# Loading and checking a GNN stack's first adjacency tiles in pieces, and reading the outcome of the check at the end

## The reference

```
layer 0: x <- norm(x + sum_k T_k(A) x w_k(node) + b(node)),  T_0 = 1, T_1 = A, T_2 = 2AA - 1,
         w_k(node) = sum_d emb[node, d] W[d, k],  b(node) = sum_d emb[node, d] bias[d],  d < 16
layer 1: x <- norm(x + relu(A relu(A x w1) w2))
layer 2: x <- norm(x + x ws + (A x) wn + bias)
layer 3: x <- norm(x + [x, Ax, 2AAx - x, Ax, 2AAx - x] W + bias)
```

## Time and profile before

| what | value |
|---|---|
| median of the runs | 1294.76 us |
| profiled execution: its own time / its span | 1295.21 us / 1293.3 us |
| TensorE matmul (PE) busy | 1258.5 us, 97% of the span |
| VectorE (DVE) busy | 729.9 us, 56% |
| ScalarE (ACT) busy | 239.8 us, 19% |
| GpSimd (POOL) busy | 62.0 us, 5% |
| first product with the adjacency starts | 20.18 us |
| mean granted TensorE clock | 0.997 |

### The profile page before, as it was taken

One profiled execution on the slowest core, in us unless ns is written; L12 is line 12 of the kernel. 1 busy time (PEld: TensorE's weight loads), 2 busy tenths in 40 slices (PEclk: granted clock), 3 DMA queues, 4 the chain that ended last, 5 costly groups with the idle time before them and its releaser, 6 DMA issues.

```text
span 1293.3 us, 16451 instructions
## 1 busy us (share of the span) xinstructions
PE 1258.5 (97%) x6048; PEld 1045.5 (81%) x6048; DVE 729.9 (56%) x1811; ACT 239.8 (19%) x427; POOL 62.0 (5%) x52
## 2 busy tenths in 40 slices
PE   5999999999999999999999999999999999999996
PEld 5887878787878787778888888888888888888875
DVE  4724898777767777778624443351256245434524
ACT  5622101120111201120112121121111121221211
POOL 0000000000000000000001001000000010010000
PEclk9999999999999999999999999999999999999998
DMA  9712112111121210101000000010001000000000
GB/s 361 290 65 85 26 53 72 43 61 37 54 61 37 59 33 20 54 21 42 14 1 1 2 1 1 1 62 5 1 24 43 1 1 1 2 1 1 33 1 35
DMA packets 27509, 55.08 MB, mean 43 GB/s; under 512 B 3472, under 2 KB 14224, under 8 KB 24976
## 3 DMA queue, kind: packets, MB, share of 16 engines
q1 hardware_dynamic: 27424, 53.96, 12.2%
HBM read 41.89 MB, written 12.06 MB: 42 GB/s over the span
## 4 chain that ended last, share of the span: by engine, by line
PE 92%; DVE 5%; ACT 1%; issue 1%; DMA 1%; SPq 0%; DVEq 0%; ACTq 0%
PE ps L594 28%; PE ps L595 28%; PE ps L703 20%; PE ps L612 7%; PE ps L633 2%; PE ps L634 2%; PE ps L606 2%; DVE nat L958 1%; DVE ring L958 1%; DVE xs L868 1%; PE ps L623 1%; ACT xs L736 1%; DMA b0t<-in_b 0%; DVE sml L900 0%; DVE sml L891 0%
## 5 line engine op out<-in xcount | busy, mean ns | idle before, releaser
L594 PE MATMUL ps<-B,xs 128*128 128x512 f32 x1664 | 658.2, 396 | 6.0 <-DVE xs L868 3.7
L595 PE MATMUL ps<-B,xs 128*128 128x512 f32 x1664 | 649.9, 391 | 0.0
L594 PEld LDWEIGHTS ps<-B,xs 128*128 128x128 f32 x1664 | 312.7, 188 | 71.1 <-issue 4.3
L595 PEld LDWEIGHTS ps<-B,xs 128*128 128x128 f32 x1664 | 312.8, 188 | 63.9
L703 PE MATMUL ps<-Tw,xs 128*128 128x512 f32 x1280 | 316.6, 396 | 2.2 <-DVE ring L958 2.2
L703 PEld LDWEIGHTS ps<-Tw,xs 128*128 128x128 f32 x1280 | 238.1, 187 | 61.4 <-DVE ring L958 4.2
L856 DVE TENSOR_TENSOR ring<-ps,rrep 128x512 f32<-128x512 f32 x94 | 64.5, 689 | 286.0 <-PE ps L595 270.0
L958 DVE SCALAR_TENSOR_TENSOR nat<-ps,embn,nat 128x128 f32<-128x128 f32 x448 | 153.7, 343 | 55.8 <-PE ps L703 55.6
L958 DVE SCALAR_TENSOR_TENSOR ring<-ps,embn,ring 128x128 f32<-128x128 f32 x512 | 175.2, 342 | 0.0
L612 PEld LDWEIGHTS ps<-W,ring 128*128 128x128 f32 x896 | 110.4, 191 | 8.0 <-DVE ring L856 3.6
L612 PE MATMUL ps<-W,ring 128*128 128x128 f32 x896 | 113.2, 275 | 2.3 <-DVE ring L856 2.3
(11 more groups left out here) (65 smaller groups left out, 623.1 us busy)
## 6 DMA issues: line engine op xcount, KB each, us to landing
raw<-in_at SPq DMA_DIRECT2D x15, 1024.0 KB, 17.2
ring<-in_xn SPq DMA_DIRECT2D x16, 256.0 KB, 2.9
ring_x<-in_xt SPq DMA_DIRECT2D x32, 128.0 KB, 3.2
ring_x<-y1d SPq DMA_DIRECT2D x32, 128.0 KB, 3.4
out<-nat SPq DMA_DIRECT2D x16, 256.0 KB, 2.1
y1d<-ring SPq DMA_DIRECT2D x14, 256.0 KB, 2.7
zd<-nat SPq DMA_DIRECT2D x12, 256.0 KB, 3.1
nat<-zd SPq DMA_DIRECT2D x3, 1024.0 KB, 4.8
```

Of the source, the lines that this page charges most:

```text
L594: pe.matmul(bank, x[:, 0, m, :], of, start=m == 0, stop=False)
L595: mm = pe.matmul(bank, x[:, 1, m, :], of, start=False, stop=ends and m == NT - 1)
```

## The change

Three tables of pieces are new: tile 0 has four, tile 1 two, tile 15 four (as before); COUNT numbers their counters. SyncE now issues `embt` and `b0t` first, then x's chunk 0, then tile 0's pieces, each with the piece of the diagonal of the same columns behind it, then tile 1's two halves, then the whole tiles. The constants follow tile 6. ScalarE, VectorE and TensorE treat a piece as a tile: the product of chunk c waits for the piece that holds it. In the first pass the two pairs alternate chunk by chunk (tile 15 keeps the pair order). TensorE's bias matmuls stay first on TensorE but use banks 3 and 7, and the copy out of PSUM, now in two halves, comes on ScalarE behind tile 0; only the products of chunk 3 wait for it. The step "branch" becomes "outcome": VectorE makes the flag there, and no engine waits for it. Each engine runs its whole list and reads the flag behind it, SyncE before its last four stores; for 0 there is nothing left but these stores.

```
+PIECES = {0: 4, 1: 2, LAST: 4}
+COUNT = [sum(PIECES.get(i, 1) for i in range(m)) for m in range(17)]
     def head():
-        put("bias")
         for m in range(NT):
...
-            for c in range(NC if m == LAST else 1):
+            for c in range(PIECES.get(m, 1)):
                 put("tile", 0, 0, c, m)
-            for j in range(2):
-                for c in range(NC if j == 0 else 2 if m >= 12 else NC):
-                    put("first", j, 0, c, m)
+            if m == 0:
+                put("bias")
+            of = [(j, c) for c in range(NC) for j in range(2) if j == 0 or c < 2 or m < 12]
+            for j, c in sorted(of) if m == LAST else of:
+                put("first", j, 0, c, m)
...
-                put("branch")
+                put("outcome")
                 put("weights0")
...
# TensorE
-                    if s.kind == "bias" and not general:
+                    if s == STEPS[0] and not general:
                         pe.wait_ge(s_e, 32)
...
-                        pe.wait_ge(s_B, tile_at[Step("tile", 0, 0, c if k == LAST else 0, k)])
-                        if k == 0:
-                            pe.wait_ge(s_b0c, 1)
+                        pe.wait_ge(s_B, tile_at[Step("tile", 0, 0, c * PIECES.get(k, 1) // NC, k)])
+                        if k == 0 and c == 3:
+                            pe.wait_ge(s_b0c, 2)
# ScalarE
-                        ac.copy(bcopy[:], ps[:, 6:8, :].rearrange("p a b -> p (a b)")).then_inc(s_b0c, 1)
+                        for i in range(2):
+                            ac.copy(bcopy[:, i * 512:(i + 1) * 512], ps[:, 3 + 4 * i, :]).then_inc(s_b0c, 1)
# VectorE, step "tile"
-                        dv.wait_ge(s_r, 16)
+                        for i in range(NC) if k else [c]:
+                            dv.wait_ge(s_r[i], 16)
# SyncE
+                sp.dma_start(embt_s, embt).then_inc(s_e, 16)
+                sp.dma_start(b0t[:], b0).then_inc(s_e, 16)
+                for m in range(NT):
+                    if m % 4 == 0:
+                        for j in range(2):
+                            sp.dma_start(ch(nat[j], m // 4), xn[j, :, m * P:(m + 4) * P]).then_inc(s_x[m // 4], 16)
+                    for c in range(PIECES.get(m, 1)):
+                        cols = piece(m, c)
+                        sp.dma_start(raw[:, m, cols], at[m * P:(m + 1) * P, cols]).then_inc(s_at[m][c], 16)
+                        if m == 0:
+                            sp.dma_start(rrep[:, cols], rb[:, cols]).then_inc(s_r[c], 16)
+                    if m == 6:
...                  the three constants
# TensorE's program; ScalarE's, VectorE's and GpSimd's likewise
-                fast.pe(eng, STEPS[:BRANCH + 1])
+                fast.pe(eng, STEPS)
                 eng.wait_ge(s_flag, 1)
                 v = eng.value_load(flag[0:1, 0:1], min_val=0, max_val=N)
-                with eng.If(v == 0):
-                    fast.pe(eng, STEPS[BRANCH + 1:])
-                with eng.Else():
+                with eng.If(v != 0):
...                  the general way
# SyncE's program
-                fast.sp(eng, STEPS[:BRANCH + 1])
+                fast.sp(eng, STEPS[:END])          # END: the first store of pair 1's output
...
                 with eng.If(v == 0):
-                    fast.sp(eng, STEPS[BRANCH + 1:])
+                    fast.sp(eng, STEPS[END:])
```

More of the change, by code:

```diff
@@ L291 @@
 SECOND = STEPS.index(Step("W"))
-BRANCH = STEPS.index(Step("branch"))
+END = STEPS.index(Step("out", 1))
 def numbered(*kinds, last=False):
@@ L385, in way @@
             if general:
-                s_g = [sem(f"load{i}") for i in range(2)]
+                s_g, s_en = [sem(f"load{i}") for i in range(2)], sem("en")
                 s_gB, s_glo, s_gmm, s_ones = sem("B"), sem("glo"), sem("mm"), sem("ones")
             else:
-                s_at = [sem(f"at{m}") for m in range(NT - 1)] + [[sem(f"at{LAST}{c}") for c in range(NC)]]
-                s_e, s_b0, s_r = sem("embt"), sem("b0"), sem("r")
+                s_at = [[sem(f"at{m}{c}") for c in range(PIECES.get(m, 1))] for m in range(NT)]
+                s_r = [sem(f"r{c}") for c in range(NC)]
+                s_e, s_b0 = sem("embt"), sem("b0")
                 s_b0c, s_nz, s_B, s_chk, s_bad, s_row = (
@@ L515, in way, with piece @@
                         held_q[n] = (s_var, var_at[Step("deviate", s.j, s.p, s.c)])
+            def piece(k, c):
+                width = N // PIECES.get(k, 1)
+                return slice(c * width, (c + 1) * width)
             def ch(t, c):
@@ L619, in pe_steps @@
                     y = y_slot(j, p, c)
-                    if s.kind == "bias" and not general:
+                    if s == STEPS[0] and not general:
                         pe.wait_ge(s_e, 32)
                         for t in range(NT):
-                            mm = pe.matmul(ps[:, 6 + t // 8, (t % 8) * C:(t % 8 + 1) * C], embt_s[:, t * P:(t + 1) * P],
+                            mm = pe.matmul(ps[:, 3 + t // 8 * 4, (t % 8) * C:(t % 8 + 1) * C], embt_s[:, t * P:(t + 1) * P],
                                            b0t[:], start=True, stop=True)
@@ L719, in act_steps @@
                         ac.wait_ge(s_b0, 1)
-                        ac.copy(bcopy[:], ps[:, 6:8, :].rearrange("p a b -> p (a b)")).then_inc(s_b0c, 1)
+                        for i in range(2):
+                            ac.copy(bcopy[:, i * 512:(i + 1) * 512], ps[:, 3 + 4 * i, :]).then_inc(s_b0c, 1)
                     if s.kind == "tile" and not general:
-                        cols = slice(c * 512, (c + 1) * 512) if k == LAST else slice(0, N)
-                        ac.wait_ge(s_at[k][c] if k == LAST else s_at[k], 16)
+                        cols = piece(k, c)
+                        ac.wait_ge(s_at[k][c], 16)
                         if tile_at[s] > 2:
@@ L834, in dve_steps @@
                         dv.wait_ge(s_const, 48)
-                        dv.tensor_tensor(odd[:, 0:NT + 3], cnt[:, 0, :], cnt[:, 1, :], ALU.not_equal).then_inc(s_chk, 1)
-                        dv.tensor_scalar(odd[:, NT + 3:], r16s[:], 0.0, None, ALU.is_equal, ALU.bypass).then_inc(s_chk, 1)
+                        dv.tensor_tensor(odd[:, 0:COUNT[NT]], cnt[:, 0, :], cnt[:, 1, :], ALU.not_equal).then_inc(s_chk, 1)
+                        dv.tensor_scalar(odd[:, COUNT[NT]:], r16s[:], 0.0, None, ALU.is_equal, ALU.bypass).then_inc(s_chk, 1)
                         dv.wait_ge(s_chk, 2)
                         dv.tensor_reduce(bad[:], odd[:], axis=AX.X, op=ALU.add).then_inc(s_bad, 1)
-                    if s.kind == "branch" and not general:
+                    if s.kind == "outcome" and not general:
                         dv.wait_ge(s_row, 16)
@@ L945, in dve_steps @@
                         if p == 0 and k == 0:
-                            dv.wait_ge(s_c2, 48)
+                            dv.wait_ge(*((s_en, 16) if general else (s_c2, 48)))
                             dv.wait_ge(s_lx[c % 2], lx_at[Step("loadx", j, 0, c)])
@@ L1138, in _ @@
             def _(eng):
-                fast.act(eng, STEPS[:BRANCH + 1])
+                fast.act(eng, STEPS)
                 eng.wait_ge(s_flag, 1)
                 v = eng.value_load(flag[0:1, 0:1], min_val=0, max_val=N)
-                with eng.If(v == 0):
-                    fast.act(eng, STEPS[BRANCH + 1:])
-                with eng.Else():
+                with eng.If(v != 0):
                     eng.copy(sml[:, 0, 0, 0, 0:1], epst[:]).then_inc(s_here, 1)
@@ L1150, in _ @@
             def _(eng):
-                fast.dve(eng, STEPS[:BRANCH + 1])
+                fast.dve(eng, STEPS)
                 eng.wait_ge(s_flag, 1)
                 v = eng.value_load(flag[0:1, 0:1], min_val=0, max_val=N)
-                with eng.If(v == 0):
-                    fast.dve(eng, STEPS[BRANCH + 1:])
-                with eng.Else():
+                with eng.If(v != 0):
                     eng.memset(bad[:], 0.0).then_inc(s_here, 1)
@@ L1163, in _ @@
             def _(eng):
-                fast.pool(eng, STEPS[:BRANCH + 1])
+                fast.pool(eng, STEPS)
+                eng.wait_ge(s_flag, 1)
+                v = eng.value_load(flag[0:1, 0:1], min_val=0, max_val=N)
+                with eng.If(v != 0):
+                    eng.memset(worst[:], 0.0).then_inc(s_here, 1)
+                    slow.pool(eng, STEPS)
+            @block.sync
+            def _(eng):
+                fast.sp(eng, STEPS[:END])
                 eng.wait_ge(s_flag, 1)
@@ L1167, in _ @@
                 with eng.If(v == 0):
-                    fast.pool(eng, STEPS[BRANCH + 1:])
-                with eng.Else():
-                    eng.memset(cnt[:, 0, 0:1], 0.0).then_inc(s_here, 1)
-                    slow.pool(eng, STEPS)
-            @block.sync
-            def _(eng):
-                fast.sp(eng, STEPS[:BRANCH + 1])
-                eng.wait_ge(s_flag, 1)
-                v = eng.value_load(flag[0:1, 0:1], min_val=0, max_val=N)
-                with eng.If(v == 0):
```

(2 more changed lines are left out.)

19 lines of the change are left out of this document (8 added, 11 removed).

## The result

The changed kernel takes 1286.26 us (median of 4 runs, 1285.87 to 1288.33) against 1294.62 us before: ratio 0.9938, 95% interval 0.9921 to 0.9955, 8.4 us less. Forecast were 1284.5 us with a range of 1281.8 to 1288.2, so direction and range held; the saving was 8.4 us in place of the 10.25 of the sum, and the time lies just above the narrower range of 1283.2 to 1286.0. The profiled execution is the longest of the four (1288.33 us, span 1286.5); a later profile of the same kernel (experiment 3) is the usual case (1286.34 us, span 1284.5).

The account below looks back on a forecast made before the run. TensorE, busy 97% of the span, was taken as the bound, so only its idle or slow time counts. 1295.21 - 7.9 (head) - 2.35 (branch) = 1284.96 us profiled, 1284.5 as median; range 1281.8 to 1288.2, narrower 1283.2 to 1286.0.

Parts of the forecast that it names:

- the sum: Whole kernel: 7.9 us from the head and 2.35 us from the branch off 1295.21 us, giving 1284.96 us.
- The start: Head of TensorE's line: first product at 11.3 us in place of 20.18, 8.9 us sooner.
- What is late next: First pass at tile 2: ready at 22.4 us, TensorE waits about 1 us, so the head saves 7.9 us.
- lands at 17.6: Tile 2's load in the head: landing at 17.6 us, with 0.3 us added for rows of 2 KB.
- rival (b): Head loads: SyncE's issuing becomes the bound, tile 2 lands 2 to 4 us later, 1286.5 to 1288.5 us; chance 0.14.
- Tile 1: First pass: second half through VectorE at 17.7 us, TensorE in tile 0 until at least 17.5.
- The branch: TensorE's idle time at the branch near 100 us goes: 2.35 us saved and kept.
- rival (d): At the branch: another wait takes its time, so only the head's saving remains, 1286.9 us; chance 0.05.
- The end: Kernel's end: VectorE's reading of the flag is covered by the last store's landing, cost 0.
- Rival (c): Kernel's end: VectorE's reading and jump outlast the last store by 1 to 3 us, 1285.5 to 1287.5 us; chance 0.07.
- The clock: First products after the bias matmuls: by the skill's rule perhaps none slow, by the rows 14 at about 0.43 us.
- rival (e): Head: start-stop keeps the clock at 1.2 GHz, 51 more slow matmuls use up the 10.25 us saved; chance 0.03.

Follow-up runs that it names:

- experiment 3: The changed kernel run and profiled once more, nothing altered: 1286.11 us.
- experiment 4: The changed kernel, but the first product waits for all four pieces of tile 0: 1286.09 us.
- 7: The changed kernel with tiles 2 and 3 loaded in halves too and tile 15 in one piece: 1285.43 us.
- experiment 6: The changed kernel, but behind the first 512 columns of tile 0 and the diagonal the other 1536 of each come in one DMA: 1285.24 us.
- Experiment 12: The changed kernel, but ScalarE issues the diagonal's four pieces as its first work, beside SyncE's issues of the rest: 1284.0 us.
- Experiment 2: The kernel before with only the branch changed (old head, outcome read behind the last step): 1292.05 us, ratio 0.9980.
- experiment 1: The changed kernel's new head with the old branch halfway through the second pass: 1288.99 us, ratio 0.9961.
- experiment 9: The changed kernel with tile 0, tile 1 and the diagonal loaded by one DMA each, checks still in pieces: 1284.75 us, ratio 0.9919.

## Why the prediction was right, and which term was mis-sized

- **The start.** Forecast 11.3 us, measured 10.70 and 10.93. The bias matmuls started at 3.68 (I had 4.2) and took 7.09 us; they were the bound, as forecast, since `B`'s first piece was there at 10.4. Right.
- **What is late next.** That tile 2's arrival takes over, and that part of the early start comes back as a wait, was right, and experiment 4 shows it. The step that was mis-sized is "lands at 17.6", with 0.3 us added for rows of 2 KB, so 17.9. It landed at 19.66 and 19.00. The chain behind it was right: 4.47 us forecast, 24.15 - 19.66 = 4.49 measured. So tile 2 began at 24.15 and 23.49 in place of 22.4, and by the usual profile the head saved 77.42 - 70.77 = 6.65 us in place of 7.9.
- **Its cause** is half found. I counted landing times back, at 2.45 us a MB, from a queue of DMAs of 1 MB each. Pieces from the one queue did not keep that pace: SyncE's issues took 0.43 us each up to 5.4 us, as I had it, but the next one 2.10 us (1.68 in experiment 3, 1.00 in 4, 0.71 in 7), and tile 2 was issued at 9.41 where I had 6.9.

```profile
9.41 10.22 DMA raw<-in_at
```

That is rival (b)'s late supply in a smaller size, by a hold and not by its 0.8 us an issue. But SyncE had not run out of bytes to offer. By 5.4 us it had issued 2.2 MB, and by 8 us only 1.3 MB had been moved (159 GB/s over 8 us), so nearly 1 MB was waiting while 144 GB/s were moved. In experiment 6, 2.8 MB had been issued by 4.4 us and 1.4 MB moved by 8 us, and the rate from 6 to 8 us was 214 GB/s. Nor does a held issue alone make the rate low: in the kernel before, two of the tiles' issues take 2.23 us together from 3.99 on, at 369 GB/s from 6 to 8 us. What limits the one queue there, and why an issue is held, was not found. Whole tiles and a second queue both bring the rate back; the first changes rows too, the second leaves them and changes who issues, and puts the diagonal's DMAs ahead of x's. Experiment 12 rules out the size of the rows. Whether it was the second queue or the earlier diagonal was not tested apart.
- **The base of the sum.** I took the old head from one profile, 77.42 with 14 slow products. Experiment 2 has the old head too, and there the transposes come at 76.56, with 9 slow ones. Against that the head saves 5.8 us, near the 5.7 between medians. So "saves 7.9" came out between 5.7 and 6.65, and the range, not the sum, took that in; with a branch worth 2.7 in place of 2.35 the total ended 1.8 us above the forecast.
- **Tile 1.** I expected no wait, and this was wrong. TensorE came sooner (start 0.6 us early, 11 or 8 slow products in place of 14) and the halves later, so 1.67 and 1.50 us were lost there; experiment 4 shows that this cost nothing by itself, because tile 2 bound behind it.
- **The branch.** Forecast 2.35; 2.53 in the profile, 2.7 in experiment 2. Right, and rival (d) did not come: in experiment 2 the branch's time does not come back elsewhere.
- **The end.** Forecast 0; 0.2 to 0.3 us measured, with a last store that took 0.4 us more. Rival (c), and with it a fetch of about 2 us put behind VectorE's reading, did not come; whether anything was fetched under the cover of the store no run shows.
- **The clock.** The bias matmuls kept TensorE busy right up to the first product in the two profiles of the changed kernel, and 11 and 8 products were slow all the same; over all kernels it was 7 to 15. By the rule of the Trainium skill that the prediction cites (TensorE: Matmul & The Clock Gate, Part 1) there might have been none, so for these small matmuls the measurement goes against it, and the 14 of the rows was the better guide. That the bias matmuls themselves ran at 1.2 GHz, as I wrote, no row shows: the granted clock of 6 to 16 us stands at 1.00, as it does over the first slow products. A waiting TensorE can lose the level again: one of the three profiles with both waits (the changed kernel's two and experiment 1's) shows it, and it cost 1.6 us there.
- **Slower than before**, rival (e), needed 51 more slow products; there were at most 5 (11 and 8 in the first profile, against 14).

## What to carry to other kernels

When a start is moved forward, find what arrives next and count from its landing: here 3.4 us of the earlier start could be given away for nothing. Cutting a load into pieces can cost more in the rate than it gains at the start, so look at the GB/s of the first few us. The two lowest medians here were those of a kernel that checks in pieces what is loaded whole (1284.75 us) and of one that issues the pieces from two engines (1284.0 us). A wait of all engines for an outcome that is nearly always the same belongs where another wait covers it.

## What the runs showed of the hardware that was not expected

- The first us are slow for the DMA engines in every kernel: 231 GB/s at a share of 1.01 from 4 to 6 us before the change, 144 to 182 in 6 to 8 us in the four profiles with the changed kernel's loads (the two of it, experiments 1 and 4), 214 and 272 in experiments 6 and 7, about 400 later. What sets it was not found.
- One queue moved only 214 GB/s from 6 to 8 us although at least 1.4 MB of what it had been given was still to be moved (experiment 6).
- DMAs of 32 partitions with rows of 8 KB, eight in a row, moved 201 GB/s from 6 to 8 us at a share of 0.94: half the rate of DMAs of 128 partitions with the same rows (397).
- The number of products at the lower clock after the bias matmuls differed from 7 to 15 between profiles, with the same 32 matmuls ahead of them (7 in experiment 12, 15 in experiment 9, where TensorE had been idle for 2.54 us).
